# Two product-key heads computed densely instead of one, with their table rows streamed, as heads 6 and 7 of eight

## What is computed

```python
kv_scores, indices = _pk(x, Wq_pk, pk_keys)      # 16 best of 64 x 64 keys, per token and head
ind = indices + offsets[None, None, :, None]     # 8 heads of 4096 rows each
k = jnp.einsum('bnhk,bnhkd->bnhd', kv_scores, keys_table[ind])
v = jnp.einsum('bnhk,bnhkd->bnhd', kv_scores, values_table[ind])
sim = jnp.einsum('bihd,bjhd->bhij', q, k)
sim = jnp.where(causal, sim, neg)
attn = jax.nn.softmax(sim, axis=-1)
out = jnp.einsum('bhij,bjhd->bhid', attn, v)
```

## Time and profile before

| | us |
|---|---|
| median of 3 runs | 6171.2 (6161.56 to 6183.76) |
| the profiled execution, its own time | 6186.85 |
| its span, first to last instruction | 6185.1 |
| busy: TensorE, VectorE, ScalarE, GpSimd | 3905.8, 3369.8, 2373.5, 4070.1 |
| first gather of table rows starts | 1477.9 |
| last gather of table rows starts | 6106.7 |

### The profile page before, as it was taken

The page is one execution under the profiler, slowest core; times in us unless marked ns, Lnnn a source line. Parts: engine busy times, 40 slices in busy tenths (PEclk is TensorE's granted clock), DMA queues, the critical chain, the costliest instruction groups (busy, mean ns, idle before and its releaser), DMA issues.

```text
span 6185.1 us, 60232 instructions
## 1 busy us (share of the span) xinstructions
PE 3905.8 (63%) x16810; PEld 2352.6 (38%) x16810; DVE 3369.8 (54%) x11755; ACT 2373.5 (38%) x6190; POOL 4070.1 (66%) x3966
## 2 busy tenths in 40 slices
PE   3659997975556665566556565665656565666456
PEld 1227774432323333333333333333333333333334
DVE  5657774427755555555555555555555555555311
ACT  1236673322333434343434344343433333333322
POOL 6117882003577777777777777777777777777773
PEclk8557776655677777777777777777777777777776
DMA  1000001231122222222222222222222222222221
GB/s 31 12 13 24 24 19 34 80 104 40 53 55 55 55 63 56 55 55 63 55 55 56 67 56 56 63 56 56 56 63 55 56 55 55 56 52 52 52 53 28
DMA packets 214358, 315.92 MB, mean 51 GB/s; under 512 B 104191, under 2 KB 143684, under 8 KB 214032
## 3 DMA queue, kind: packets, MB, share of 16 engines
q0 software_dynamic: 118784, 239.31, 15.6%
q1 hardware_dynamic: 95248, 72.84, 3.8%
HBM read 279.39 MB, written 32.52 MB: 50 GB/s over the span
## 4 chain that ended last, share of the span: by engine, by line
POOL 56%; issue 17%; DVE 3%; PE 2%; ACT 0%; DMA 0%; POOLq 0%; DVEq 0%
POOL sq_rows L1794 56%; PE sq_ps_d L1818 1%; DVE sq_d_negmax L2103 0%; PE sq_ps_c L1841 0%; PE sq_ps_o L1860 0%; DVE sq_scratch L2196 0%; DVE sq_row_f L2198 0%; DVE sq_scratch L2194 0%; PE sq_ps_v L1884 0%; ACT sq_ps_d L1992 0%; DVE sq_sim_rest L2153 0%; DVE sq_top_at L2154 0%; PE sq_ps_t L1849 0%; DVE sq_stack L2219 0%; DVE sq_top_at L2165 0%
## 5 line engine op out<-in xcount | busy, mean ns | idle before, releaser
L1794 POOL DMA_INDIRECT sq_rows<-in_L_ffn_table,sq_row x3584 | 3501.1, 977 | 1224.8 <-issue 1091.7
L2059 ACT ACTIVATE sq_rows<-sq_rows,sq_weight 128x128 f32<-128x128 f32 x3584 | 1070.3, 388 | 2070.6 <-DMA sq_rows<-in_L_ffn_table,sq_row 2070.6
L1884 PE MATMUL sq_ps_v<-sq_rows,sq_ident 128*128 128x512 f32 x1792 | 1179.3, 818 | 831.8 <-ACT sq_rows L2059 831.8
L2317 DVE TENSOR_REDUCE sq_kv<-sq_ps_v 128x128 f32<-128x512 f32 x224 | 154.9, 692 | 1914.8 <-PE sq_ps_v L1884 1914.8
L1884 PEld LDWEIGHTS sq_ps_v<-sq_rows,sq_ident 128*128 128x128 f32 x1792 | 463.5, 273 | 1400.7 <-issue 1400.7
L1939 PE MATMUL sq_ps_z<-sq_stackT,sq_spread 128*128 128x128 bf16 x3072 | 357.2, 265 | 538.7 <-DVE sq_kv L2265 480.1
L1939 PEld LDWEIGHTS sq_ps_z<-sq_stackT,sq_spread 128*128 128x128 bf16 x3072 | 273.6, 121 | 629.9 <-DVE sq_kv L2265 519.7
L1818 PE MATMUL sq_ps_d<-sq_d_q,sq_d_k 64*128 64x512 f32 x512 | 351.8, 773 | 72.8 <-ACT sq_ps_d L1992 65.3
L999 POOL TENSOR_TENSOR at_psum_p<-at_prob 128x1024 f32<-128x1024 f32 x128 | 301.6, 2361 | 136.1 <-ACT at_prob L957 136.1
L859 DVE CUSTOM_DVE_ANT_1 at_att<-at_ps_att,at_bias 128x1024 f32<-128x1024 f32 x256 | 306.8, 1218 | 119.1 <-PE at_ps_att L1051 108.0
L1949 PE MATMUL sq_ps_z<-sq_dense_table,sq_dense_w 128*128 128x128 f32 x2048 | 319.1, 304 | 22.8 <-DVE sq_dense_w L2253 22.1
(11 more groups left out here) (366 smaller groups left out, 7153.2 us busy)
## 6 DMA issues: line engine op xcount, KB each, us to landing
sq_rows<-in_L_ffn_table,sq_row POOLq DMA_INDIRECT x3584
qkvT<-exp_rows SPq DMA_DIRECT2D x32, 768.0 KB, 3.3
sq_d_q<-qkvT SPq DMA_DIRECT2D x8, 1024.0 KB
sq_d_k<-qkvT SPq DMA_DIRECT2D x32, 256.0 KB
sq_d_v<-qkvT SPq DMA_DIRECT2D x32, 256.0 KB
at_parts_dram<-at_parts SPq DMA_DIRECT2D x8, 384.0 KB, 2.3
at_qS<-at_parts_dram SPq DMA_DIRECT2D x48, 64.0 KB, 2.3
at_kS<-at_parts_dram SPq DMA_DIRECT2D x48, 64.0 KB, 2.4
```

Of the source, the lines that this page charges most:

```text
L1794: pool.indirect_dma_start(rows[v % GSLOTS][:, k, :], None, w2["table"], bass.IndirectOffsetOnAxis(row[tile % 3][:, h, k:k + 1], 0)).then_i ...
L1884: mm = pe.matmul(ps_v[:, :], ident[:, :], slot[:, 4 * k:4 * k + 4, :].rearrange("p k c -> p (k c)"), start=(k == 0), stop=(k == TOPK // 4 ...
L2059: ins = act.activation(slot[:, k, :], slot[:, k, :], ACT.Copy, scale=weight[tile % 3][:, h, k:k + 1])
```

## The change

A second head is computed densely. `DENSE` becomes `(6, 7)`, so each tile has six gathered heads (0 to 5, `GATHERED`) and two steps without a gather. Each step now has two dense pieces, one for each dense head (numbered c = 2g and 2g + 1). The table of the dense heads no longer stays in SBUF: each piece's rows (128 partitions by 4 blocks by 128 numbers) are loaded by SyncE from a copy laid out for it (`dense_rows`) into one of six buffers (`chunk`), two steps ahead. There are five gather buffers instead of four. The loop bodies are rearranged: on TensorE one dense multiplication opens the step and the other stands between `mix` and the second spread; ScalarE's second exponential follows `weigh`; the codes of a tile's dense heads are built by VectorE in steps 1 to 4 of the tile before, one of four in each step (`dense_codes`), instead of in steps 6 and 7. The build sets `dynamic_dma_scratch_size=8192`, which it did not set before.

```diff
-GSLOTS = 4
-DENSE = HEADS2 - 1
+GSLOTS = 5
+DENSE = (6, 7)
+ND = len(DENSE)
+GATHERED = [h for h in range(HEADS2) if h not in DENSE]
+NG = len(GATHERED)
+CHUNKS = 6
...
-        dense_table = sb("dense_table", [P, NBLOCKS, KV])
+        chunk = [sb(f"chunk{k}", [P, PER_STEP, KV]) for k in range(CHUNKS)]
...
+                def load_chunk(c):
+
+                    if c >= CHUNKS:
+                        sp.wait_ge(S["dense_ps"], c - CHUNKS + 1)
+                    sp.dma_start(chunk[c % CHUNKS][:, :, :], w2["dense_rows"][c % ND, c // ND % HEADS2]).then_inc(chunk_in[c % CHUNKS], 16)
...
# TensorE
+                    if 0 <= g - 1 < ALL:
+                        dense_values(ND * g - 1)
+                    if h == 0 and 0 <= slot < NTILES:
+                        dense_transposes(slot)
...
+                    if 0 <= g < ALL:
+                        dense_spread(ND * g)
...
+                    if 0 <= g - 1 < ALL and (g - 1) % HEADS2 not in DENSE:
+                        mix(g - 1)
                     if 0 <= g < ALL:
-                        dense_spread(g)
-                    if 0 <= g - 1 < ALL and (g - 1) % HEADS2 != DENSE:
-                        mix(g - 1)
+                        dense_values(ND * g)
+                        dense_spread(ND * g + 1)
...
# ScalarE
                     if 0 <= g < ALL:
-                        dense_exponentials(g)
+                        dense_exponentials(ND * g)
...
-                    if 0 <= g < ALL and h != DENSE:
+                    if 0 <= g < ALL and h not in DENSE:
                         weigh(g)
+                    if 0 <= g < ALL:
+                        dense_exponentials(ND * g + 1)
...
# VectorE
+                    if 0 <= g - 1 < ALL:
+                        dense_weights(ND * g - 1)
                     if d < ALL:
                         diagonal_unit(d)
+                    if 0 <= w < ALL:
+                        causal_max(w)
...
+                    if 0 <= g - 1 < ALL:
+                        dense_sum(ND * g - 1)
+                    if h == 0 and 0 <= slot < NTILES:
+                        s.wait()
+                        dense_split(slot)
                     if 0 <= chosen < NTILES:
                         choose(chosen, 2 * h)
...
+                    if 0 <= g < ALL:
+                        dense_weights(ND * g)
+                    if 0 <= g - 1 < ALL and (g - 1) % HEADS2 not in DENSE:
                         store_mix(g - 1)
                     if 0 <= g < ALL:
-                        dense_weights(g)
+                        dense_sum(ND * g)
+                    if 0 <= chosen < NTILES and 2 * h + 1 < 13:
+                        choose(chosen, 2 * h + 1)
+                    if 1 <= h <= 2 * ND and 0 <= slot + 1 < NTILES:
+                        dense_codes(slot + 1, h - 1)
...
-    nc = bacc.Bacc("TRN2", target_bir_lowering=False, num_devices=1)
+    nc = bacc.Bacc("TRN2", target_bir_lowering=False, num_devices=1, dynamic_dma_scratch_size=8192)
```

More of the change, by code:

```diff
@@ L1559, in gather_unit @@
 def gather_unit(u):
-    return u // HEADS2 * DENSE + u % HEADS2
+    return u // HEADS2 * NG + sum(h < u % HEADS2 for h in GATHERED)
 def sequence_pipeline(nc, w1, w2, qkvT, h_in, h_out):
@@ L1668, in sequence_pipeline @@
         d_kv_in = [sem(f"d_kv_in{k}") for k in R]
+        chunk_in = [sem(f"chunk_in{k}") for k in range(CHUNKS)]
         dve_steps = sem("dve_steps")
@@ L1735, in _ @@
                 dve.wait_ge(gp_made, 4)
-                dve.tensor_copy(head_base[:, :], row[0][:, 0, 0:HEADS2])
+                for v, h in enumerate(GATHERED):
+                    dve.tensor_copy(head_base[:, v:v + 1], row[0][:, 0, h:h + 1])
                 dve.tensor_copy(number[:, :], row[1][:, 0:4, :].rearrange("p a b -> p (a b)")).then_inc(gp_made, 1)
@@ L1794, in _ @@
                         pool.indirect_dma_start(rows[v % GSLOTS][:, k, :], None, w2["table"],
-                                                bass.IndirectOffsetOnAxis(row[tile % 3][:, h, k:k + 1], 0)).then_inc(gathered[v % GSLOTS], 16)
+                                                bass.IndirectOffsetOnAxis(row[tile % 3][:, v % NG, k:k + 1], 0)).then_inc(gathered[v % GSLOTS], 16)
             @block.tensor
@@ L2232, in dense_stack, with dense_codes @@
                     s.wait()
                     dve.sem_inc(S["sim_used"], 1)
-                    dve.sem_inc(S["stack_ready"], 1)
+                def dense_codes(tile, part):
+                    i, second = divmod(part, 2)
+                    s.wait()
+                    s.did(dve.tensor_tensor(is_key, bc(number[:, :], 1, TOPK), bc(kept_at[:, i, second, :], 2, NKEYS), ALU.is_equal))
+                    s.wait()
+                    s.did(dve.tensor_tensor(is_key, is_key, bc(code_of_rank[:, :] if second else row_count[:, i, :], 2, NKEYS), ALU.mult))
+                    s.wait()
+                    s.did(dve.tensor_reduce(stack[tile % 2][:, i, 1, 1 - second, :], is_key.rearrange("p k c -> p c k"), AX.X, ALU.add))
+                    if part == 2 * ND - 1:
+                        s.wait()
+                        dve.sem_inc(S["stack_ready"], 1)
@@ L2255, in dense_sum @@
                 def dense_sum(c):
-                    tile, part = divmod(c, HEADS2)
-                    to = kv[tile // TT % 2][:, tile % TT, :, DENSE, :]
+                    tile, part = divmod(c // ND, HEADS2)
+                    h = DENSE[c % ND]
+                    to = kv[tile // TT % 2][:, tile % TT, :, h, :]
                     ps = ps_z[:, 0:KV].rearrange("p (m c) -> p m c", m=2)
@@ L2376 @@
         + ["L1_attn_" + n for n in "Wqkv_heads bqkv_heads W0_heads b0".split()]
-        + ["L1_ffn_" + n for n in "Wq_pkT keysT Wq table Wo".split()])
+        + ["L1_ffn_" + n for n in "Wq_pkT keysT Wq table dense_rows Wo".split()])
 def build(nc, a, out):
```

155 lines of the change are left out of this document (74 added, 81 removed).

## The result

The changed kernel takes 6018.07 us in the median of four runs (6006.85 to 6043.92); the kernel before took 6168.17 beside it (6161.56 to 6183.76). The ratio is 0.9759 [0.9722, 0.9796]: faster by 2.4%, or 150 us. The forecast was 5766, a gain of 6.5%. The sign was right and the time is inside the range; the forecast time was 252 us too low.

The account below looks back on a forecast made before the run. GpSimd's gathers bound the old kernel; afterwards the dense chain would, at 131 us a tile plus 2 for the clock. Span 1524 + 32 x 133 = 5780, becoming 5766 us as median; range 5530 to 6165, chance 0.70.

Parts of the forecast that it names:

- The chain through three engines: Spread, exponential, dense_weights, multiplication, sum: goes round twice a step through TensorE, ScalarE and VectorE; VectorE's waits 36.7 us a tile.
- The formula, span = 1524 + 32 T: Whole run: 1583 before the first dense exponential, 32 tile periods T, 65 after the last step, less 124 for lighter tiles.
- 131 us at the full clock: Tile period at the full TensorE clock: 94.5 us of VectorE work plus 36.7 us of waits, above GpSimd's 123.
- The hand count of VectorE's work: VectorE's work in a tile, added up in order with gaps between dependent instructions: 94.5 us.
- I allow 2 us [for the clock] and take 133.: Allowance per tile for a TensorE clock not always full, raising the period from 131 to 133 us.
- The step followed: Step 3 of a tile, traced: 16.5 us, VectorE working 11.4 and waiting 5.1, TensorE finished at about 13.5.
- The clock rule of the Trainium skill: TensorE: activity releases the throttled default clock; by that alone the period would be 131, 64 us less over the run.
- The rival of the low clock: TensorE waits of 4 us ending steps 1 to 4 drop the clock: 36 us a tile, T = 167, 6850 us; chance 0.07.
- GpSimd stays the bound: Waits overestimated by over a fifth, T below 125.5, gathers decide: span 5535, time 5521 us; chance 0.20.
- The gather gets dearer: Smaller scratch or chunk loads slow GpSimd's gathers: it decides from 1.39 us, gain gone at 1.52; chance 0.03.
- SBUF copies and gathers: Added VectorE copies may hold GpSimd's port, adding a few us a tile to gathers; GpSimd-bound rival then about 5580.
- The cover of the chunk loads: SyncE's chunk loads, asked for about two steps (30 us) ahead, cost nothing; failure would show as TensorE waiting on chunk.

Follow-up runs that it names:

- the filler: The changed kernel plus sixteen extra TensorE multiplications at the start of steps 2 to 5, their result overwritten by mix: 5767.16 us, ratio 0.9335.
- the tables moved: The changed kernel with VectorE's code tables in steps 1 to 4 built behind the first sorting piece, not at the step's end: 5572.3 us, ratio 0.9026.

## Why the prediction was right in kind and wrong in size

- **GpSimd was the bound, and its relief was real.** Right in kind. Its waits for `mix` were to be 300 us and were 480.7. ScalarE's wait for rows was to shrink to a small part of 2070.6, and no idle time is left before `weigh`.
- **The chain through three engines sets the period.** Right: the changed kernel gains nothing when half the gathers are withheld, and 520 us when VectorE's tables are left out.
- **The formula, span = 1524 + 32 T.** It holds for the changed kernel: with the 140.4 us measured it gives 6017 us, 12 above the span of 6005.0. It isn't general. With the periods of the filler, of the tables moved and of the tables moved with half the gathers (131.9, 124.6, 117.6) it gives 5745, 5511 and 5287, where the spans were 5774.3, 5561.7 and 5362.3. What the constant lacks there is open.
- **131 us at the full clock.** Supported by the run with the filler: 131.9, and step by step within 0.7 us, except for step 0, which took 13.6 instead of 12.4 us in both kernels. The clock there was 0.89, so what a full clock in every step would give is not shown. The hand count of VectorE's work, 94.5, was 94.75 in the tile shown.
- **"I allow 2 us [for the clock] and take 133."** This is the term that failed. It cost 7 to 9 us: TensorE's own work was 239 us longer than with the filler, 7.5 a tile, and the periods differ by 8.5. The span was 225 us above the forecast's 5780, and the period 7.4 us above 133, which is 237 us in 32 tiles. The other 27 of the 252 us are no mechanism: the forecast took the median to lie 14 us below the profiled execution's span, as before, and it lay 13 above it. I had put the clock between two rows, 1.00 at 12.0 of 14 us busy and 0.72 at 7.1 of 14, and had read it by the busy share of the whole step. The idle time isn't spread over the step: it is one gap of 4.7 to 5.2 us at its end, and the first multiplication and spread, the fourth layer's products and a good part of `mix` come right behind it, with the chain waiting for them. They run at the low clock, whatever the mean says. The step followed had the gap in it ("TensorE finished at about 13.5 and stood idle"), and the rival named it.
- **The clock rule of the Trainium skill.** By the Trainium skill, TensorE: Matmul & The Clock Gate, Part 1: The HAM clock gate, activity should have released the clock, and the sum would have been 131. TensorE got busier, from 2748 of 4629 us to 3152 of 4424, and the granted clock rose only from 0.74 to 0.80. The direction agrees. What I had made of it, that a busier TensorE holds the full clock, does not hold here; with more activity in the gap the clock rose to 0.89, and the period was 131.9.
- **The rival of the low clock** had the mechanism: its gaps of 4 us "at the end of steps 1 to 4" measured 4.7 and 5.2 where shown. Its size was too big (36 us a tile, where 8 were paid), since the clock comes back within `mix` and the loss is in three steps, not in all. It and the forecast were one mechanism of two sizes, and the truth lay between.
- **GpSimd stays the bound**: fell for the kernel as changed, and came true, 27 us above its own figure, once the tables were moved.
- **The gather gets dearer**: no. Its mean went from 0.977 to 0.991 us, 1.4%. The scratch plays no part that shows; the chunks were not tested by themselves.
- **SBUF copies and gathers.** The code tables, two for each dense head and tile, are no copies but two `tensor_tensor` and one `tensor_reduce` each. With them left out, the mean gather was 967 ns instead of 993. The trace of the changed kernel shows which gathers are the slow ones. Between 1600 and 5400 us, 663 gathers overlap a `tensor_tensor` of VectorE on `sq_scratch`, SBUF to SBUF, nearly all for code tables or row numbers: their mean is 1.123 us, and 210 took over 1.1. Of the other 1940, 2 did, and their mean is 0.946, also beside the `tensor_reduce` (0.945). One such:

```profile
3673.84 1.47 POOL L1813 DMA_INDIRECT sq_rows<-in_L_ffn_table,sq_row  x1 [0.30 <-issue]
3674.52 1.23 DVE L2257 TENSOR_TENSOR sq_scratch<-sq_scratch,sq_row_count 128x1024 f32<-128x1024 f32 x1
```

The run with the heads at 3 and 7 has the same tables and a mean of 975: only 539 of its gathers fall beside such an instruction. The Trainium skill, SBUF — State Buffer, Who interferes with whom, says that VectorE copies can, in some modes, keep GpSimd from writing descriptors, and that a `tensor_tensor` with both inputs in SBUF contends with GpSimd's reads but was not seen to stall a DMA. Here it went with slower gathers, so on that last point the measurement decides. That a port is the cause was not tested.

- **The cover of the chunk loads held.** TensorE never waited for a chunk: its idle time before the multiplications is put down to `dense_weights` for 939.2 of 939.7 us, while the DMA engines went from 22% to 30% busy.

The 656 us that the missing gathers could have brought divide as follows. 150 were gained. 251 went with the clock that falls in the gap (the filler brings them back). Another 195 lie between the run with the filler and the one with the tables moved: there the tables' place makes the chain the bound at 132 us a tile, 7 above the 124.6 that GpSimd allows. The last 60 are missing with the tables moved too.
